# Scores for the attention maxima: sixteen row-strip matmuls instead of four with a block-diagonal K

## What is computed

```
Q = split(layernorm(x) @ Wq.T, 16 heads of 32);  K = V = split(ctx @ Wq.T)
attn = softmax(Q K^T / sqrt(32)) over 77 keys
x = x + (attn V) @ Wo.T
x = x + ffn(layernorm(x))      # gate, up, down with fake int8 quantisation by global maxima
```

## Time and profile before

| | us |
|---|---|
| median of 3 runs | 1266.21 (1264.27 to 1271.19) |
| the profiled execution | 1264.66 |
| its span | 1262.5 |
| PE busy | 1160.0 (92%) |
| DVE busy | 888.7 (70%) |
| ACT busy | 683.2 (54%) |
| PE matmul group Q, L655 | 195.8 for 768 |
| PE matmul group O, L699 | 183.6 for 720 |
| exponential on ACT, L556 | 120.1 for 64 |

### The profile page before, as it was taken

The page is one execution under the profiler, slowest core; times in us unless marked ns, Lnnn a source line. Parts: engine busy times, 40 slices in busy tenths (PEclk is TensorE's granted clock), DMA queues, the critical chain, the costliest instruction groups (busy, mean ns, idle before and its releaser), DMA issues. The chain is left out here.

```text
span 1262.5 us, 18613 instructions
## 1 busy us (share of the span) xinstructions
PE 1160.0 (92%) x6716; PEld 667.1 (53%) x6764; DVE 888.7 (70%) x1591; ACT 683.2 (54%) x829; POOL 120.6 (10%) x80
## 2 busy tenths in 40 slices
PE   6458899999999999999999939999999999699888
PEld 5345566666666666666666424444444444244333
DVE  5866577777777777777766556787787878575565
ACT  5744655555555555555554514665656555754450
POOL 0100000000000000000000000000000000165677
PEclk9769999999999999999999978999999999799999
DMA  9841122223222232221111264554545510499977
GB/s 354 321 153 43 51 76 79 89 76 111 76 76 90 87 111 76 76 76 67 59 52 51 84 221 179 199 205 191 216 180 194 213 71 35 205 400 420 415 288 274
DMA packets 77364, 196.86 MB, mean 156 GB/s; under 512 B 5895, under 2 KB 12807, under 8 KB 71279
## 3 DMA queue, kind: packets, MB, share of 16 engines
q1 hardware_dynamic: 77295, 195.94, 42.9%
HBM read 119.02 MB, written 76.90 MB: 155 GB/s over the span
## 5 line engine op out<-in xcount | busy, mean ns | idle before, releaser
L655 PE MATMUL a_Q<-a_xnT,wq 128*128 128x512 f32 x768 | 195.8, 404 | 8.7 <-DVE a_xnT L640 7.7
L862 ACT ACTIVATE e_sg<-e_G,x_gus 128x512 f32<-128x512 f32 x176 | 119.1, 685 | 134.4 <-PE e_G L962 134.4
L655 PEld LDWEIGHTS a_Q<-a_xnT,wq 128*128 128x128 f32 x768 | 140.8, 190 | 86.7 <-issue 58.0
L699 PE MATMUL a_O<-a_wo,a_aT 128*128 128x512 f32 x720 | 183.6, 403 | 0.0
L962 PE MATMUL e_G<-e_cT,e_gu 128*128 128x512 bf16 x686 | 179.9, 382 | 2.7 <-DVE e_cT L908 1.8
L921 DVE SCALAR_TENSOR_TENSOR h<-e_U,x_gus,e_sg 128x512 f32<-128x512 f32 x176 | 131.3, 748 | 70.9 <-PE e_U L966 43.3
L966 PE MATMUL e_U<-e_cT,e_gu 128*128 128x512 bf16 x689 | 179.6, 381 | 0.8
L1101 PE MATMUL c_Y<-dn,c_cb 128*128 128x512 bf16 x689 | 157.6, 389 | 18.0 <-DVE c_cb L1064 17.0
L699 PEld LDWEIGHTS a_O<-a_wo,a_aT 128*128 128x128 f32 x720 | 130.6, 188 | 46.5 <-issue 19.2
L556 ACT ACTIVATE a_pr<-a_S 77x2048 f32<-77x2048 f32 x64 | 120.1, 1876 | 26.4 <-PE a_S L677 26.4
L1101 PEld LDWEIGHTS c_Y<-dn,c_cb 128*128 128x128 bf16 x704 | 69.9, 100 | 105.7 <-issue 16.6
(11 more groups left out here) (138 smaller groups left out, 1361.3 us busy)
## 6 DMA issues: line engine op xcount, KB each, us to landing
x<-x_d SPq DMA_DIRECT2D x32, 1024.0 KB, 7.1
h_d<-h SPq DMA_DIRECT2D x24, 1024.0 KB, 3.9
h<-h_d SPq DMA_DIRECT2D x11, 1536.0 KB, 18.6
a_xr<-in_x SPq DMA_DIRECT2D x64, 256.0 KB, 2.8
x_d<-a_xr SPq DMA_DIRECT2D x64, 256.0 KB, 2.0
out<-c_y SPq DMA_DIRECT2D x15, 1024.0 KB, 10.9
xa<-in_x SPq DMA_DIRECT2D x56, 256.0 KB, 2.7
h<-h_d SPq DMA_DIRECT2D x11, 1280.0 KB, 15.4
```

What stands on the lines that cost most here:

```text
L655: mm = nc.tensor.matmul(Q[:], wq[:, wp, j, P * n.g:P * (n.g + 1)], xnT[:, n.par, xp, j], start=(ins == 0), stop=(ins == 3 * KT - 1))
L699: mm = nc.tensor.matmul(projection(n), aT[:, n.par, ap, j, P * n.g:P * (n.g + 1)], wo[:, wp, j], start=(ins == 0), stop=(ins == 3 * KT - 1))
L862: nc.scalar.activation(sg[:, s], G[:, t % GU], ACT.Silu, scale=gus[:, t:t + 1]).then_inc(silued, 1)
```

## The change

The four matmuls of 308 columns become sixteen of 78 columns: for each of the four token tiles, four heads, each on its own strip of 32 rows, into four PSUM banks. They read K from `kt`, which the column scores use too, padded from 77 to 78 keys (`KW`) with a zero column. `kbd`, its mask, its sixteen copies, its stores and its loads go. S now holds [head][tile][78] for the maxima instead of [tile][head][77].

TensorE's turn becomes: column scores of item k-2, Q of k+4, transposes of the maxima (in turns k % 4 = 1), scores for the maxima of k+3, O of k-7, transposes of x for k+8, denominators and then values of k-2. Everything behind the column scores lies one turn later, and there is one more turn in all. Denominators signal `summed`, and the reciprocal waits for that instead of for the values; it is written over its own logarithm. The ring of Q buffers grows from 6 to 7.

On ScalarE the exponential comes right behind the reciprocal, and the normalising of x behind the copy of Q. On VectorE the maximum reduction moves from the front to behind the subtraction for the attended part and the copy of the turned maxima, ahead of the subtraction for Q.

```diff
+KW = KEYS + 1
 # prepare
-        kbd = sb("p_kbd", [P, GROUPS, BATCH, HG, KEYS], F32R)
+        zero = sb("p_zero", [P, 2 * GROUPS * BATCH])
-                for g in range(GROUPS):
-                    sp.wait_ge(s_kbd, g + 1)
-                    w = HG * KEYS
-                    sp.dma_start(kbd_d[:, :, w * g:w * (g + 1)].rearrange("b p n -> p b n"),
-                                 kbd[:, g].rearrange("p b h k -> p b (h k)").bitcast(F32)).then_inc(s_out, 16)
+                sp.wait_ge(s_pad, 2)
+                nc.gpsimd.memset(zero[:], 0.0).then_inc(s_pad, 1)
+                pool.wait_ge(s_pad, 1)
+                nc.gpsimd.tensor_copy(kt[:, :, :, :, KEYS], zero[:].rearrange("p (b s g) -> p b s g", b=BATCH, s=2)).then_inc(s_pad, 1)
-                act.wait_ge(in_id, 32)
-                for g in range(GROUPS):
-                    act.wait_ge(s_kt, g + 1)
-                    for j in range(HG):
-                        ins = nc.scalar.activation(kbd[:, g, :, j], kt[:, :, 0, g].bitcast(F32), ACT.Copy, scale=hmask[:, j:j + 1])
-                    ins.then_inc(s_kbd, 1)
 # attend
-RINGQ = 6
+RINGQ = 7
-        SLOTS = range(FIRST, STEPS + 8)
+        SLOTS = range(FIRST, STEPS + 9)
-            return Q if k >= 6 else O if k >= 0 else (O, A, DN)[k % 3]
+            return Q if k >= 7 else O if k >= 0 else (O, A, DN)[k % 3]
 # ScalarE
-                    done = at(k, -2)
+                    done = at(k, -3)
...
-                        act.wait_ge(valued, done.n + 1)
+                        act.wait_ge(summed, done.n + 1)
+                        after(act, att_rdy, done.n)
...
+                    now = at(k, -2)
+                    if now:
+                        act.wait_ge(scored, now.n + 1)
+                        after(act, valued, now.n)
+                        nc.scalar.activation(pr[:], S[0:KEYS], ACT.Exp, scale=SM_SCALE).then_inc(exped, 1)
 # VectorE
-                        nc.vector.tensor_reduce(mx5[:, :, :, n.g], S[:, :, 0:HG * KEYS].rearrange("p t (h k) -> p t h k", h=HG),
-                                                AX.X, ALU.max).then_inc(maxed, 1)
+                        nc.vector.tensor_reduce(mx5[:, :, :, n.g].rearrange("p t h -> p h t"),
+                                                S[:, :, 0:TT * KW].rearrange("p h (t k) -> p h t k", t=TT)[:, :, :, 0:KEYS],
+                                                AX.X, ALU.max).then_inc(maxed, 1)
...
                         dve.wait_ge(rcp_rdy, done.n + 1)
+                        dve.wait_ge(valued, done.n + 1)
 # TensorE, column scores moved to the front of the turn, then Q, then
+                    if (n := at(k, 3)):
+
+                        after(pe, exped, n.n - 4)
+                        after(pe, maxed, n.n)
+                        if n.n % PER == 0:
+                            pe.wait_ge(k_in[n.batch % 2], 16 * (n.batch // 2 + 1))
+                        pe.wait_ge(qT_h, n.n + 1)
+                        for t in range(TT):
+                            for h in range(HG):
+                                rows = slice(DH * h, DH * (h + 1))
+                                mm = nc.tensor.matmul(S[:, h, KW * t:KW * (t + 1)], qT[rows, n.ring, 0, P * t:P * (t + 1)],
+                                                      kt[rows, n.batch % 2, 0, n.g], start=True, stop=True)
+                        mm.then_inc(m_scored, 1)
...
-                    if (n := at(k, 4)):
-
-
-                        after(pe, exped, n.n - 4)
-                        after(pe, maxed, n.n)
-                        if n.n % PER == 0:
-                            pe.wait_ge(kbd_in[n.batch % 2], 16 * (n.batch // 2 + 1))
-                        pe.wait_ge(qT_h, n.n + 1)
-                        for t in range(TT):
-                            mm = nc.tensor.matmul(S[:, t, 0:HG * KEYS], qT[:, n.ring, 0, P * t:P * (t + 1)],
-                                                  kbd[:, n.batch % 2, n.g], start=True, stop=True)
-                        mm.then_inc(m_scored, 1)
                     if now:
...
                         for h in range(HG):
-                            nc.tensor.matmul(A[DH * h:DH * (h + 1)], v[:, now.batch % 2, P * now.g + DH * h:P * now.g + DH * (h + 1)],
-                                             pr[:, h], start=True, stop=True)
+                            mm = nc.tensor.matmul(DN[DH * h:DH * (h + 1)], ones[:], pr[:, h], start=True, stop=True)
+                        mm.then_inc(summed, 1)
                         for h in range(HG):
-                            mm = nc.tensor.matmul(DN[DH * h:DH * (h + 1)], ones[:], pr[:, h], start=True, stop=True)
+                            mm = nc.tensor.matmul(A[DH * h:DH * (h + 1)], v[:, now.batch % 2, P * now.g + DH * h:P * now.g + DH * (h + 1)],
+                                                  pr[:, h], start=True, stop=True)
                         mm.then_inc(valued, 1)
```

More of the change, by code:

```diff
@@ L452, in attend @@
         kv_in = [sem(f"a_kv_in{p}") for p in range(2)]
-        kbd_in = [sem(f"a_kbd_in{p}") for p in range(2)]
+        k_in = [sem(f"a_k_in{p}") for p in range(2)]
         (w_in, c_in, w_split, consts, mx_zero, ve_rdy, r0_rdy, rs_rdy, normed, transposed, xnT_h, xnT_l,
-         q_done, qT_h, qT_l, scored, m_scored, maxed, m_turned, mT_rdy, exped, valued, ln_done,
+         q_done, qT_h, qT_l, scored, m_scored, maxed, m_turned, mT_rdy, exped, summed, valued, ln_done,
          rcp_rdy, att_rdy, aT_h, aT_l, projected, x1_rdy, mom_rdy, own_d, own_a) = (sem("a_" + n) for n in (
@@ L553, in _ @@
                         nc.scalar.activation(qT[:, n.ring, 0], Q[:], ACT.Copy).then_inc(qT_h, 1)
-                    if (n := at(k, -1)):
-                        act.wait_ge(scored, n.n + 1)
-                        nc.scalar.activation(pr[:], S[0:KEYS], ACT.Exp, scale=SM_SCALE).then_inc(exped, 1)
+                    n = at(k, 8)
+                    for g in (range(TT) if k == -8 else () if not n or k < -4 else (n.g,)):
+                        if g == 0:
+                            act.wait_ge(rs_rdy, n.block + 1)
+                        t = xa[:, n.par, g]
+                        nc.scalar.activation(t, t, ACT.Identity, bias=nb[:, g:g + 1], scale=rs[:, g:g + 1]).then_inc(normed, 1)
                     if k % 4 == 3 and (n := at(k, 12)):
@@ L645, in _ @@
                 for k in SLOTS:
+                    now = at(k, -2)
+                    if now:
+                        after(pe, maxed, now.n + 5)
+                        after(pe, exped, now.n)
+                        pe.wait_ge(mT_rdy, now.block + 1)
+                        pe.wait_ge(qT_l, now.n + 1)
+                        if now.n == 0:
+                            pe.wait_ge(consts, 2)
+                        if now.n % PER == 0:
+                            pe.wait_ge(kv_in[now.batch % 2], 16 * (now.batch // 2 + 1))
+                        for kp, qp in ((0, 0), (0, 1), (1, 0)):
+                            for h in range(HG):
+                                rows = slice(DH * h, DH * (h + 1))
+                                nc.tensor.matmul(S[0:KEYS, h], kt[rows, now.batch % 2, kp, now.g, 0:KEYS], qT[rows, now.ring, qp],
+                                                 start=(kp + qp == 0), stop=False)
+                        for h in range(HG):
+                            rows = slice(DH * h, DH * (h + 1))
+                            mm = nc.tensor.matmul(S[0:KEYS, h], negw[rows, now.g], mT[rows], start=False, stop=True)
+                        mm.then_inc(scored, 1)
                     if (n := at(k, 4)):
-                        turned = n.n + 4 if k > 6 else n.n - n.g + 4
+                        turned = n.n + 4 if k > 7 else n.n - n.g + 4
                         after(pe, xnT_h, turned)
@@ L658, in _ @@
                         mm.then_inc(q_done, 1)
-                    now = at(k, -1)
-                    if now:
-                        after(pe, maxed, now.n + 5)
-                        after(pe, exped, now.n)
-                        pe.wait_ge(mT_rdy, now.block + 1)
-                        pe.wait_ge(qT_l, now.n + 1)
-                        if now.n == 0:
-                            pe.wait_ge(consts, 2)
-                        if now.n % PER == 0:
-                            pe.wait_ge(kv_in[now.batch % 2], 32 * (now.batch // 2 + 1))
-                        for kp, qp in ((0, 0), (0, 1), (1, 0)):
-                            for h in range(HG):
-                                rows = slice(DH * h, DH * (h + 1))
-                                nc.tensor.matmul(S[0:KEYS, h], kt[rows, now.batch % 2, kp, now.g], qT[rows, now.ring, qp],
-                                                 start=(kp + qp == 0), stop=False)
-                        for h in range(HG):
-                            rows = slice(DH * h, DH * (h + 1))
-                            mm = nc.tensor.matmul(S[0:KEYS, h], negw[rows, now.g], mT[rows], start=False, stop=True)
-                        mm.then_inc(scored, 1)
```

(14 more changed lines are left out.)

100 lines of the change are left out of this document (40 added, 60 removed).

## The result

Median 1272.26 us (20 runs) against 1268.22 for the kernel before (20 runs). The ratio is 1.003, 95% interval 1.0018 to 1.0042: slower by 0.3%, less than the 0.5% I had called the limit of what can be told, and still clear of noise with 20 runs of each. The forecast was 1270, slower by 0.3%. So the two traces differ by 10 us of span where the medians differ by 4, and a sum made from them has to say which part repeats.

A forecast was written before the change was run, and what follows sets the result against it. TensorE's own order and work bound the loop. Preparation counted nothing; lead-in, full turns and run-out reached 726.4 against 722.2, less 0.7: +3.5 us, giving a median of 1270 us, range 1256 to 1290.

The forecast's parts named there:

- The maxima scores are a wash: Loop, TensorE: sixteen strip matmuls take 0.60 us with load-bound rounds of 0.11, replacing 0.57.
- Rival B: Maxima scores: 78 columns go at the plain f32 pace, stretch 0.78 us, +10.7 us, 1280; chance 0.22.
- C: Maxima scores: a strip's next weights do not load during its matmul, round 0.16, +8.4 us, 1278; chance 0.05.
- F: Maxima scores: strips do not run side by side, stretch 1.9 us, +78 us, 1348; chance 0.02.
- E: Maxima scores: a round's four loads cost less than one full load, stretch 0.30 us, -18 us, 1252; chance 0.16.
- A full turn takes 9.92: Steady loop turns: by medians 9.92 us against 9.89 before, +0.03, with TensorE never waiting.
- rival D: Loop: transposes of x wait for VectorE's subtraction for Q behind the reduction, +20 us, 1290; chance 0.11.
- The removed preparation is worth nothing: Preparation: dropping sixteen ScalarE copies and four stores saves nothing; the stage still ends at 62.0 us.
- Lead-in: a turn of 5.8 us at full clock: Loop's start: Q, maxima scores, reduction and subtraction follow one another, 5.8 us a turn; first column scores at 117.3.
- Turns without O: 8.02: Five turns before output products start: 8.02 us each instead of 8.72, transposes of x waiting for copy and normalising.
- Run-out +5.4: Loop's last turns: one of 8.55 us, five of 5.94 and 0.44 more; this stretch grows by 5.4 us.
- Denominators first save 0.7 behind the last turn: After the loop: the 0.59 us wait behind the first last output product goes, with 0.1 of switching: -0.7.

The follow-up runs named there:

- experiment 8: Changed kernel with each strip matmul streaming 128 columns of K instead of 78; one execution, 0.60 us from maxima scores to output product.
- experiment 5: Changed kernel plus 40 filler matmuls where TensorE waits in the lead-in; ratio 1.0009 to the kernel before, median 1268.78 us.
- experiment 9: Kernel before with strip maxima scores in its old order, plus 40 filler matmuls in turns 1 to 5; ratio 0.9984, median 1266.84 us.
- experiment 3: Changed kernel with ScalarE's normalising of x moved ahead of its copy of Q; ratio 0.9984 to the kernel before, median 1267.42 us.
- experiment 7: Changed kernel with block-diagonal maxima scores, normalising ahead of the copy of Q, and subtraction ahead of the reduction before turn 2; ratio 0.9829, median 1246.33 us.
- experiments 1 to 4: Four runs sharing one chip and its executions of the kernel before; the fourth is the changed kernel unaltered, ratio 1.0033.
- experiment 2: Changed kernel's new order with the old block-diagonal full-array maxima scores; ratio 0.9912 to the kernel before, median 1257.93 us.
- experiment 1: Kernel before with only the maxima scores changed to sixteen strip matmuls, old order kept; ratio 1.0042, median 1273.18 us.

## Why the prediction was right, and where it was not

- *The maxima scores are a wash.* Right: 0.57 against my 0.60, and load-bound rounds of 0.11. Rival B is excluded by experiment 8, C by the rounds of 0.11 where it wanted 0.16, F by the same rows. E would have needed less than 0.44. (E's 0.30 is a little low by the forecast's own terms: with rounds and a first load of 0.04 they give 0.32.)
- *A full turn takes 9.92.* It took 9.89, so that 53 of them gave back 1.9 us more. TensorE is busy for 528.01 of 528.01 us, so rival D did not happen. (T lay at 7.54 by the forecast's own terms, not 7.58, and came at 7.50.)
- *The removed preparation is worth nothing.* Nothing was gained. The stage ended 1.0 us later (63.0 against 62.0). In the seven traces with this preparation it ended between 61.5 and 65.1, in the five with the old one between 62.1 and 62.8, so the 1.0 lies within the scatter of one preparation.
- *Lead-in: a turn of 5.8 us at full clock.* This term was mis-sized: first column scores at 123.2, not 117.3. All 5.9 arose behind the second Q. The first came 1.0 late but was shorter (4.52 for 5.46), so that the second stood where I had it, 85.61 for 85.65; then four Q products took 17.95 us together, 5.9 more than at 3.02 each. I had read the level in the earlier trace rows for the first Q and then let it be full for good, because in the kernel before it was full from 84 us on. My own schedule had stretched the lead-in with waits, and I did not ask whether the clock would survive them. That the low level was the loss, and not the waits by themselves, experiments 5 and 9 show: they leave every wait in the code and only add work, and the lost time comes back.
- *Turns without O: 8.02.* Measured 8.03 from one column score to the next. The 0.44 added for turning the maxima was not paid, since T waits that much less there (0.53 for 0.96): five turns took 40.2 against 40.5. The mechanism (normalising, then T) was right, as experiment 3 shows by taking it away.
- *Run-out +5.4.* +6.0. The 0.6 are two waits in the turn that turns the last maxima, which I had taken as free.
- *Denominators first save 0.7 behind the last turn.* They saved nothing: the wait before the last output products is 0.58, as in the earlier trace rows. VectorE's timeline of the changed kernel shows the statistics of x1, 1.6 us, between the division and the subtraction that releases them (L586). The subtraction begins 2.2 us behind the division, where it was 1.4 before, and that took the time back:

```profile
731.29 0.69 DVE L564 TENSOR_TENSOR a_att<-a_A,a_lnd 128x512 f32<-128x512 f32 x1 [1.54 <-ACT a_lnd L520]
731.90 0.69 DVE L579 BATCH_NORM_STATS2 a_bst<-a_xr 128x6 f32<-128x512 f32 x1
...
733.51 0.69 DVE L586 TENSOR_TENSOR a_aT<-a_att,a_aT 128x512 fp32r<-128x512 f32 x1
```

The forecast of the total was closer than its parts deserve: it was 5.6 too small for the stretch before the full turns in this trace and 1.9 too large for them, and it was compared with medians that lie nearer to each other than the two profiled executions. Between the traces it was 6.1 too small (1274.3 against 1268.2); that it met the medians within 2.3 us, and the 0.3% exactly, is luck. Why the medians lie nearer is open in part. The executions of the kernel before spread over 11 us (1263.16 to 1274.24) and those of experiment 7 over 2 (1245.51 to 1247.72, six runs). Time and granted clock go together there: of the 28 of the kernel before beside experiments 1 to 4, the seven with a mean of 0.968 or more took 1261.3 to 1267.2 us, the four with 0.961 or less 1270.1 to 1272.3. That its lead-in, too, loses the clock in some executions would fit both, but in which stretch those executions lost it, no trace here shows.

## To carry to other kernels

Before replacing few wide matmuls by many narrow ones on strips, count the weight loads and the ways in and out of the strip form: here they made up for all that was saved, and keeping one more stage in the full-array form was worth 0.22 us a turn, 1.2% in all, once the order had put it between two other full-array stages. In the old order it was worth nothing in a turn. A schedule made by hand at full clock is a lower bound where TensorE waits; look at the granted clock of each sparse stretch, and when a new order adds waits there, price the matmuls behind them at the low level as well. Pipeline edges deserve an order of their own: two instructions moved for their sake (experiments 3 and 7) took the median from 1257.9 to 1246.3, about as much again as the new order by itself had brought (experiment 2).

## What the runs showed of the hardware

- The low level can come and go within a lead-in: with 28.75 us of work in 40 the clock averaged 0.83, with 36.53 it was 1.00, and a Q product took 4.4 to 4.6 us in place of 3.0. The work in a stretch does not tell the level by itself: the kernel before had 1.00 with 32.10 and with 33.48, experiment 1 had 0.83 with 34.88. Adding 40 useless matmuls to experiment 1 took the ratio from 1.0042 to 0.9984 (experiment 9), and 40 in the changed kernel took 5.4 us out of its lead-in and 3 to 4 us off its time, the latter at the edge of the noise (experiment 5). I had not expected that added work could pay.
- Loads for four row strips run side by side also at 128 columns each: sixteen in 0.53 us, four rounds 0.11 apart. And f32r matmuls of 78 and of 128 columns on strips hide beneath them: the fifty columns more cost 0.023 us in all.
- Going from the full array to row strips and back costs 0.22 us, as experiment 2 has it beside the changed kernel: 0.08 in the Q product ahead (2.95 for 2.87), 0.14 in the O product behind (2.90 for 2.76).
